# A four-layer network on one core: moving work about in the stretch ahead of a 512-step recurrence

## The reference, cut to what matters

```python
# layer 0: which 5120 entries of a batch's 512 x 512 are largest, as ones
adj = fside * cond[:, None, :] * softmax(x) * 512 ** -0.5; adj[diagonal] = -inf
x = x + ones_at(top_k(adj.reshape(4, -1), 5120))        # ties go to the lowest index
# layer 1: attention, 16 heads of 32
scale, shift = split(cond @ W_emb + b_emb)
xn = rms_norm(x, g_norm) * (1 + scale) + shift
q, k, v = heads(xn @ W_qkv); q, k = rms_norm(q, g_q), rms_norm(k, g_k)
o = softmax(q @ k.T * 32 ** -0.5) @ v
x = x + o + o @ W_out
# layer 2: a GRU over the 512 rows, first state cond
x = x + gru(cond, x, W_ih, W_hh, b_ih, b_hh)
# layer 3: linear sampling of x along the features at places given by cond
x = x + sample(x, cond)
```

## Time and profile before

| | |
|---|---|
| median of 3 timed runs | 2341.22 us (2340.92 to 2341.77) |
| profiled execution: its time, its span | 2339.34 us, 2337.6 us |
| TensorE busy | 93% of the span |
| VectorE, ScalarE, GpSimd busy | 67%, 54%, 22% |
| granted TensorE clock | 0.991 of full over the span |
| x of batch 0 in | 6.32 us |
| first ranking (L956) | 40.03 us |
| last bound of the search done | 136.90 us |
| first projection of batches 0 to 3 | 169.19, 318.59, 471.48, 625.85 us |
| first step of the recurrence | 808.98 us |

### The profile page before, as it was taken

The page is one execution under the profiler, slowest core; times in us unless marked ns, Lnnn a source line. Parts: engine busy times, 40 slices in busy tenths (PEclk is TensorE's granted clock), DMA queues, the critical chain, the costliest instruction groups (busy, mean ns, idle before and its releaser), DMA issues.

```text
span 2337.6 us, 132042 instructions
## 1 busy us (share of the span) xinstructions
PE 2184.3 (93%) x56213; PEld 1850.2 (79%) x56213; DVE 1562.3 (67%) x7116; ACT 1272.9 (54%) x5557; POOL 506.9 (22%) x2267
## 2 busy tenths in 40 slices
PE   3778999898988999999999999999999999999998
PEld 2664655545545699999999999999999999999886
DVE  7986866778668456666666666666666667666665
ACT  5754946747548454566544445445454555444443
POOL 2001121121120122233222222222222222222221
PEclk9999999999999999999999999999999999999999
DMA  5000000010010000000000000000000000000000
GB/s 200 3 2 0 1 1 1 1 55 1 1 54 1 19 5 5 5 5 5 5 5 5 9 9 5 9 9 5 9 5 10 10 5 9 10 5 14 9 5 21
DMA packets 8404, 31.58 MB, mean 14 GB/s; under 512 B 836, under 2 KB 904, under 8 KB 7560
## 3 DMA queue, kind: packets, MB, share of 16 engines
q1 hardware_dynamic: 7392, 23.07, 2.6%
q10 hardware_dynamic: 424, 0.07, 0.0%
HBM read 18.94 MB, written 4.19 MB: 10 GB/s over the span
## 4 chain that ended last, share of the span: by engine, by line
PE 79%; DVE 12%; ACT 5%; issue 3%; POOL 0%; DMA 0%; ACTq 0%; DVEq 0%; POOLq 0%
PE psum L1710 49%; PE psum L1644 8%; PE psum L1479 5%; PE psum L1555 4%; PE psum L1573 3%; PE psum L1539 3%; PE psum L1519 2%; PE psum L1671 2%; DVE region_cols L994 2%; DVE region_cols L978 2%; DVE top L1135 1%; PE psum L1498 1%; PE psum L1457 1%; ACT region_rows L666 1%; PE psum L1588 1%
## 5 line engine op out<-in xcount | busy, mean ns | idle before, releaser
L1710 PE MATMUL psum<-parts0A,region_w_hh 128*128 128x40 f16 x12288 | 428.6, 181 | 7.9 <-DVE parts0A L1351 6.2
L1710 PE MATMUL psum<-parts1A,region_w_hh 128*128 128x40 f16 x12288 | 428.0, 181 | 6.7 <-DVE parts1A L1351 6.5
L1710 PE MATMUL psum<-parts1B,region_w_hh 128*128 128x40 f16 x12288 | 427.2, 181 | 1.3 <-issue 0.3
L1710 PE MATMUL psum<-parts0B,region_w_hh 128*128 128x40 f16 x12288 | 426.7, 181 | 0.6
L1710 PEld LDWEIGHTS psum<-parts0A,region_w_hh 128*128 128x128 f16 x12288 | 378.2, 96 | 44.3 <-DVE parts0A L1351 11.2
L1710 PEld LDWEIGHTS psum<-parts1A,region_w_hh 128*128 128x128 f16 x12288 | 377.6, 96 | 42.6 <-DVE parts1A L1351 11.6
L808 ACT ACTIVATE mixA<-rzA 128x8 f32<-128x8 f32 x512 | 110.8, 216 | 534.8 <-DVE rzA L1306 534.7
L1710 PEld LDWEIGHTS psum<-parts1B,region_w_hh 128*128 128x128 f16 x12288 | 361.6, 96 | 5.0 <-DVE parts1B L1351 1.8
L1710 PEld LDWEIGHTS psum<-parts0B,region_w_hh 128*128 128x128 f16 x12288 | 361.7, 96 | 3.5 <-DVE parts0B L1351 1.2
L486 POOL TENSOR_SCALAR lineA<-lineA 128x8 f32<-128x8 f32 x512 | 122.2, 239 | 845.0 <-DVE lineA L1342 845.0
L1306 DVE TENSOR_REDUCE rzA<-psum 128x8 f32<-128x32 f32 x512 | 97.8, 191 | 249.4 <-PE psum L1710 248.0
(11 more groups left out here) (228 smaller groups left out, 3717.4 us busy)
## 6 DMA issues: line engine op xcount, KB each, us to landing
region_rows<-in_x_dram SPq DMA_DIRECT2D x4, 1024.0 KB, 12.7
out_dram<-region_w_b SPq DMA_DIRECT2D x16, 256.0 KB, 2.4
region_w_a<-in_L_cond_W_qkv_dram SPq DMA_DIRECT2D x1, 3072.0 KB, 23.3
region_w_hh<-in_L_cond_W_hh_dram SPq DMA_DIRECT2D x4, 768.0 KB, 6.5
region_w_a<-in_L_cond_W_ih_dram SPq DMA_DIRECT2D x1, 3072.0 KB, 10.1
region_cond<-in_cond_dram SPq DMA_DIRECT2D x2, 1024.0 KB, 7.1
region_cols<-in_L_cond_W_emb_dram SPq DMA_DIRECT2D x1, 2048.0 KB, 19.0
region_w_out<-in_L_cond_W_out_dram SPq DMA_DIRECT2D x1, 1024.0 KB, 21.6
```

The costliest lines, as they stand in the source:

```text
L1710: made = e.matmul(k.slots(bank)[:, :, ch, :, 0:2], k.w16[:, 2 * read + c, part, NC * "rzn".index(g) + 2 * half + ch], k.parts[now][read][: ...
```

## The change

Ten pieces, all ahead of the recurrence:

1. `pe_embed` makes the embedding as rows (4 x 1024) with 8 program products of 512 columns, ahead of the first count; ScalarE copies them (`act_embed`) behind batch 2's keys and ahead of batch 3's; the first sum of a count waits for these copies. After the search eight transposes bring them into the old columns.
2. On SP's queue the condition rows move behind x of batch 1.
3. `dve_prepare` is split: its first three operations come ahead of the ranking, the nine scale operations behind the last masks of the search. GpSimd's all-reduce moves behind all the diagonals of v.
4. The first mask compares v with the pivot itself, in place of `side` with zero, so that only the later count waits for Sign; its prefix sums come ahead of the quota, `dve_scales` between them; and VectorE does the four last adds in place of GpSimd.
5. One-column activations (`act_table`) bring table loads forward: Sqrt behind the signs, Exp in each attention ahead of the last two turned copies, Sigmoid ahead of the recurrence.
6. `pe_columns` runs in pairs of blocks: raw, raw, normalised, normalised.
7. The diagonals have a place for each batch, and those of batches 1 to 3 are made in unit 2 of the attention before.
8. In batch 0 the value products of tiles 2 and 3 move behind the other products, each ahead of a turn of halves, and VectorE copies both behind its last low halves.
9. In batches 1 to 3 the last output product is cut in two, with the first scores between the halves, and VectorE's last output add comes behind the first maximum.
10. Batch 2's prefix sums wait for batch 1's normalised transposes, whose diagonals lie in the same place.

```diff
 def sp_program(e, k):
     e.dma_start(k.x[:, 0], ...)
-    e.dma_start(k.cond_rows.rearrange("p b d -> p (b d)"), ...)
     for b in range(1, B):
+        if b == 2:
+            e.dma_start(k.cond_rows.rearrange("p b d -> p (b d)"), ...)
         e.dma_start(k.x[:, b], ...)
...
@@ act_program
         if b:
             act_keys(e, k, b - 1, NT)
+    act_embed(e, k)
     act_keys(e, k, B - 1, NT // 2)
     act_search(e, k)
...
+    act_table(e, k, B, ACT.Sqrt)
     e.wait_ge(s["gt_sign"], B)
     act_row_powers(e, k, 0)
...
+def act_table(e, k, i, function):
+    e.activation(k.warm[:, i:i + 1], k.ones[:, 0:1], function)
+
+def act_embed(e, k):
+    for half in range(2):
+        e.wait_ge(s["emb_products"], half + 1)
+        e.activation(k.emb_rows[:, half * D:(half + 1) * D], k.banks[4 + half][0:B, :], ACT.Copy).then_inc(s["emb_rows"], 1)
...
@@ dve_program
     dve_row_max(e, k, 0)
-    dve_prepare(e, k)
     dve_row_max(e, k, 1)
...
     dve_mask(e, k, 3)
+    dve_prepare_most(e, k)
     dve_search(e, k)          # now calls dve_prepare behind its last mask
...
-    dve_mask_equal(e, k, 0); dve_mask_prefix(e, k, 0); dve_mask_quota(e, k, 0); dve_mask_taken(e, k, 0)
-    dve_scales(e, k)
+    dve_first_mask(e, k)
...
+def dve_first_mask(e, k):
+    dve_mask_equal(e, k, 0)
+    for t in range(NT):
+        e.tensor_tensor_scan(k.prefix[:, t], k.eq[:, t], ...).then_inc(s["prefix"], 1)
+    dve_scales(e, k)
+    dve_mask_quota(e, k, 0)
+    for t in range(NT):
+        e.wait_ge(s["quota"], 8)
+        e.wait_ge(s["prefix"], t + 1)
+        e.scalar_tensor_tensor(k.eq[:, t], k.prefix[:, t], k.quota[:, 0, t:t + 1], k.eq[:, t], ALU.is_le, ALU.mult).then_inc(s["taken"], 1)
+        e.scalar_tensor_tensor(k.x[:, 0, t], k.side[0][:, t], 0.0, k.x[:, 0, t], ALU.is_gt, ALU.add).then_inc(s["prefix"], 1)
+        e.wait_ge(s["taken"], t + 1)
+        e.wait_ge(s["prefix"], NT + t + 1)
+        e.tensor_tensor(k.x[:, 0, t], k.x[:, 0, t], k.eq[:, t], ALU.add).then_inc(s["masked"], 1)
...
@@ dve_attention
     if b:
         dve_out_adds(e, k, b - 1, (2,))
+    dve_maxima(e, k, b, 0)
+    if b:
         dve_out_adds(e, k, b - 1, (3,))
-    for n in range(AHEAD):
-        dve_maxima(e, k, b, n)
+    dve_maxima(e, k, b, 1)
...
+        if n == 2 and b + 1 < B:
+            dve_diagonals(e, k, b + 1)
...
@@ pe_program
     e.transpose(k.bank(7, VEC_ROWS), ...).then_inc(s["vec"], 1)
+    pe_embed(e, k)
     pe_search(e, k)
-    pe_embed(e, k)
+    pe_embed_columns(e, k)
...
 def pe_embed(e, k):
+    for half in range(2):
+        for c in range(NC):
+            made = e.matmul(k.banks[4 + half][0:B, :], k.condT[:, :, c], k.w_emb[:, c, half * D:(half + 1) * D], ...)
+        made.then_inc(s["emb_products"], 1)
...
@@ pe_attention
-        pe_project(e, k, b, t, (1, 2))
+        pe_project(e, k, b, t, (1, 2) if values_in_turn(b, t) else (1,))
         pe_turn_stack(e, k, b, t - 1, 0)
     if b:
         pe_out_matmuls(e, k, b - 1, (0,))
+    else:
+        pe_project(e, k, b, NT - 2, (2,))
     pe_turn_stack(e, k, b, NT - 2, 1)
     if b:
         pe_out_matmuls(e, k, b - 1, (1, 2))
+    else:
+        pe_project(e, k, b, NT - 1, (2,))
     pe_turn_stack(e, k, b, NT - 1, 0)
     pe_turn_stack(e, k, b, NT - 1, 1)
     if b:
-        pe_out_matmuls(e, k, b - 1, (3,))
-    for n in range(AHEAD):
-        pe_scores(e, k, b, n)
+        pe_out_matmuls(e, k, b - 1, (3,), range(0, 2))
+    pe_scores(e, k, b, 0)
+    if b:
+        pe_out_matmuls(e, k, b - 1, (3,), range(2, NC))
+    pe_scores(e, k, b, 1)
```

More of the change, by code:

```diff
@@ L275, in layout @@
         self.xT = view("cols", 0, FP32, NC, B, S)
-        self.diagonal = view("work", 24, FP32, NT, P)
+        self.diagonal = [view(*place, FP32, NT, P) for place in (("work", 24), ("w_hh", 12), ("rows", 4), ("rows", 12))]
         self.qk = view("work", 0, FP32, NT, QK, DH)
@@ L695, in act_attention @@
     act_stack(e, k, b, NT - 1, 1)
+    act_table(e, k, b, ACT.Exp)
     act_turn_stack(e, k, b, NT - 1, 0)
@@ L773, in act_gru @@
     s = k.sem
+    act_table(e, k, B + 1, ACT.Sigmoid)
     e.wait_ge(s["hh_scale"], 8)
@@ L1054, in dve_row_scales, with dve_diagonals @@
     e.reciprocal(k.row_rms[:, b], k.row_rms[:, b]).then_inc(s["row_rms"], 1)
+def dve_diagonals(e, k, b):
+    s = k.sem
+    for t in range(NT):
+        e.tensor_scalar(k.diagonal[b][:, t], k.ident[:], k.row_rms[:, b, t:t + 1], None, ALU.mult).then_inc(s["diagonals"], 1)
 def dve_columns(e, k, b):
@@ L1063, in dve_columns @@
         e.wait_ge(s["gt_sign"], B)
-    for t in range(NT):
-        e.tensor_scalar(k.diagonal[:, t], k.ident[:], k.row_rms[:, b, t:t + 1], None, ALU.mult).then_inc(s["diagonals"], 1)
     if b == 0:
+        dve_diagonals(e, k, b)
         e.wait_ge(s["row_power"], NT)
@@ L1507, in pe_out_matmuls @@
     for m in ms:
-        if b < B - 1:
+        if cs[0]:
+            pass
+        elif b < B - 1:
             n = NT * (b + 1)
@@ L1517, in pe_out_matmuls @@
             e.wait_ge(s["exp"], 2 * len(UNITS) * B)
-        for c in range(NC):
+        for c in cs:
             made = e.matmul(k.bank(m, S), k.w_out[:, c, m * P:(m + 1) * P], k.oT[:, c], start=(c == 0), stop=(c == NC - 1))
-        made.then_inc(s["w_out"], 1)
+        if cs[-1] == NC - 1:
+            made.then_inc(s["w_out"], 1)
 def pe_scores(e, k, b, n):
```

104 lines of the change are left out of this document (69 added, 35 removed).

## The result

The changed kernel takes 2316.89 us (median of 4 runs, 2313.34 to 2317.88) against 2341.07 (2339.71 to 2341.77) beside it: 0.9895 of the time before, interval 0.9878 to 0.9912. Forecast were 2312 and 2305 to 2322. Its profiled execution took 2313.34 for a span of 2311.6, 26.0 less than that of before.

What follows compares the result with a forecast made beforehand. The recurrence's products at L1710 (49% of the chain) bound the kernel, so gains lie only ahead of it: -3.2 - 6.3 - 2.3 - 9.4 + 0.9 - 8.7 = -29.0 from 2341.2, giving 2312 us; own range 2307 to 2317, with rivals 2305 to 2322.

Steps and rivals of the forecast that it cites:

- Start: Up to the first ranking: earlier weights but early embedding products, batch 3's mask at 34.8 instead of 38.18; -3.2 us.
- Search to first projection: From the search's last bit to the first projection: mask, table load and columns earlier, -6.3 us, bounds -8 and -3.5.
- The mask's term: Between search and first projection: the first mask's last tile at 154.4 against 158.2, -3.7 us, bounds -4.5 to -2.4.
- the table load's: Between squares and root after the search: ScalarE's 1.28 us load, issued behind the signs, leaves the way; -1.3.
- the columns' -1.3: First transposes to first projection: raw and normalised groups without waits, one group partly slow, 6.3 us instead of 7.56.
- Batch 0: Batch 0's projections to scores: value products fill TensorE's waits, scores start at 228.5; -2.3 us, bounds -3.5 and -0.5.
- Changes of batch: Three changes, divide to projection: early diagonals let raw and normalised groups run without a gap; -9.4 us, bounds -11 and -5.5.
- The forecast's lower bound: Changes of batch: if only the wait for diagonals goes, some 1.8 us each, -5.5 for the three.
- Starts of scores: Three starts, last output product to weighted values: half product ahead and early Exp, -2.9 each, -8.7 us, bounds -11 and -5.9.
- +0.9 for the diagonals: Unit 2 of batches 0 to 2: VectorE's four small early-diagonal passes cost 0.9 us in all, bounds 0 and 2.6.
- The signs named in advance: Profile marks: first projection near 159.7, weighted values at 15 to 15.5; wrong if products exceed 12 us or recurrence grows over 2.
- rival 4: Recurrence: gain lost through shifted code and other alignments, break-even 57 ns a step over 512 steps, 2341 us; chance 0.01.

Runs made afterwards that it cites:

- keys_first: Changed kernel with batch 3's keys ahead of the embedding copies on ScalarE; ranking 2.83 us behind the embedding products, against 3.77.
- embed_late: Changed kernel with the row-form embedding products back behind the search; ranking at 34.66, first transposes 1.55 us later, recurrence starts at 782.82.
- filled: Changed kernel plus 12 unread TensorE products ahead of batch 0's columns; ratio to the kernel before 0.9891 (0.9875 to 0.9906).
- before_again: The kernel before, unedited, profiled a second time; recurrence starts at 809.76 and lasts 1534.54 us, against 808.98 and 1528.62.
- v_in_turn: Changed kernel with batch 0's value products and copies of tiles 2 and 3 back in turn; projection to scores 62.08 us, against 60.96.
- late_exp: Changed kernel without any early Exp table load; last output product to weighted values 16.76, 15.90, 16.13 us against 15.74, 15.74, 15.30.
- late_diag: Changed kernel with diagonals of batches 1 to 3 built at the change of batch again; first change 9.00 us, against 7.35.
- v_one_late: Changed kernel with only tile 3's value product late and no early Exp in batch 0; ratio to the kernel before 0.9898 (0.9882 to 0.9913).
- pool_adds: Changed kernel with the first mask's four last adds back on GpSimd; first transposes 0.97 us later, 18.92 behind the last bound.

## Why the prediction was right, point by point

**Start, -3.2 forecast, -2.7 measured** at the ranking. The products came at 23.7 and took 9.85 (forecast 24.0 and 9), the mask at 35.23 (34.8). The step held; keys_first shows what it overlooked: of two things that ScalarE had to do at 33.6, the copies went first, and the ranking waited 0.9 longer for it. The forecast didn't part the products' new place from their new form; embed_late shows that the place gains nothing in this order.

**Search to first projection, -6.3 forecast, -4.3 measured.** The mask's term was right (-3.7, measured -3.36), and so was the table load's (-1.3, measured -1.07, from the last add to the first normalised products). The mis-sized term is the columns' -1.3: "TensorE has been at work since 154.5, so that I cost one group of L1457 slow in part (1.5)". Its parts as listed (1.5, three at 0.9, two at 0.45, 0.9) come to 6.0, not 6.3, so that the list itself gives -1.6. Two groups were slow, 3.78 for the pair, and the stage took 7.70 against 7.56 before. filled gave back 2.1 of it. By the other profiles one pair sizes it badly: 8.26 in before_again, 6.16 to 7.71 in changed kernels without fillers. The rule cited in the prediction from the Trainium skill ("TensorE: Matmul & The Clock Gate", Part 1), that the throttled state is the default and activity releases it, agrees with filled, where TensorE was at work up to the columns, and with embed_late, where it had rested 8.6 us just ahead of them and the stage took 7.63.

**Batch 0, -2.3 forecast, -0.7 measured.** "Two value products (7.0 together) go into these gaps": they did, and the wait of 5.20 before 226.10 went down to 1.48. What the step left out is the gap that they left behind: 3.76 at 196.21, and after it 1.50 and 4.94 at the slower level, 1.7 more than 1.06 and 3.65. v_in_turn puts the worth of the piece at 1.1 to the scores, and at 0.4 to the first weighted values. late_exp puts the price of the early load at 0.2: as forecast, it brings nothing here.

**Changes of batch, -9.4 forecast, -9.6 measured** (-3.74, -2.09 and -3.73). late_diag divides it: 1.65 a change for the diagonals, and a rest of 2.1, 0.4 and 2.1. The 0.4 is the pairs of blocks: with a second raw group run inside it, the wait of 1.83 for the diagonals is 1.39 in late_diag. The first normalised products of the first change, in before and in late_diag:

```profile
310.94 1.47 PE L1457 MATMUL psum<-region_work,region_rows 128*128 128x128 f32 x8 [1.83 <-DVE region_work L1065]
```

```profile
300.79 2.05 PE L1543 MATMUL psum<-region_w_hh,region_rows 128*128 128x128 f32 x16 [1.39 <-DVE region_w_hh L1120]
```

The 1.65 more in the first and third change is TensorE's level in before, which fell there behind the wait, and not in the second (windows of before, columns as in the last section):

```profile
307.50:318.60 11.10, 8.41 (x61) 7.96 (x57) 5.18 (x12) 3.71 (x5) 0.00 (x0) 0.85 0.00 0
462.04:471.48 9.44, 6.75 (x60) 6.32 (x57) 5.18 (x12) 3.71 (x5) 0.00 (x0) 1.00 0.01 2
```

In late_diag all three run at full clock although the wait is there; why it fell in two of three places before isn't shown. The forecast's lower bound, 1.8 for the wait alone, was the right size for the diagonals.

**Starts of scores, -8.7 with +0.9 for the diagonals, measured -2.4, -2.2 and -3.6.** The sum is near, -8.2 for -7.8. In batch 1 the split is worth 1.6, Exp 1.0, and the diagonals cost 0.4. "exponential at +3.9 instead of +7.2" was +4.1, the second pair's at +6.5 was +6.8, and the weighted values came at +15.7, just outside the 15 to 15.5 that were named for them, and inside in batch 3. What didn't bear out is that an early load saves its 1.28: the second unit's maximum, 1.30 late, hides most of it in batch 2 and part of it elsewhere (late_exp). The load was 1.28 long in each of these kernels, with 0.02 or less between it and a function that was ready, ahead of it too where ScalarE had been at work (143.07 in after). So the 2.66 that the Trainium skill gives a switch ("ScalarE: Activation LUTs", What ACT_TABLE_LOAD costs) has no place here.

**What wasn't forecast:** batch 3's way from projection to scores, 74.69 before, was 71.58 in after and 71.57 in v_one_late, but 72.85 to 74.54 in the nine others with the same order there; 1.4 of the gain in after's profile is up to the last output product, differs between executions of one kernel, and is luck. So is part of the total: the named stretches gave 25.3 of their 29.0, these tiles 1.3 more, the recurrence took some back, and the median of 2316.89 lies 0.1 inside the forecast's own 2307 to 2317.

**The signs named in advance.** Products of 9.85, under 12; no table load between squares and root, nor ahead of the first exponential, nor in the recurrence after its start; no pause of TensorE over 1 us behind unit 2; the last add 3.4 earlier, not 3.7; first projection 162.36, not 159.7; recurrence 0.7 longer in the first pair. By the other profiles the limit of 2 us set for it was smaller than what the same kernel does from one execution to the next (1529.28, 1536.49; before, 1528.62, 1534.54), so one pair could not have told anything. The forecast of 0 for the recurrence was wrong all the same, by some 2 us or more: the medians and the usual step say so above. It is what rival 4 named, shifted code, in a small size; that the code's place is the cause isn't shown.

## What to carry to other kernels

Undo each piece alone and read the stretch it touches, not the time: pieces worth 1 to 4 us were clear in single profiles, while five timed executions showed nothing of 3 us. But keep the sum of the stretches beside the time: where the time gains less each time, the stretch that nobody touched has changed. A load or copy moved off the way is worth what the next wait behind it leaves, so follow the chain to the second and third unit before giving it its full length. And when work leaves an engine whose clock falls at rest, price what runs behind the gap at the slower level too.

## What the runs showed of the hardware that was not expected

- The record of the granted clock starts with its first change. In before it reads 1.00 from the start, also at 161.63, where eight normalised products took 2.08 instead of 1.06; in after the same counts stand under 0.54 and 0.50, once wide products at 23.7 have lifted it. Windows of before and of after (us, busy and count of PE, PEld, DVE, ACT, POOL, then PEclk, DMA share, GB/s):

```profile
60.00:158.00 98.00, 76.17 (x1769) 67.91 (x1769) 92.68 (x146) 69.03 (x315) 5.63 (x4) 1.00 0.01 3
```

```profile
60.00:158.00 98.00, 66.61 (x1668) 58.03 (x1669) 93.02 (x163) 69.89 (x309) 0.00 (x0) 0.50 0.01 3
```

  So a mean clock of 0.991 before and 0.969 after is no slower chip: embed_late, where nothing wide runs before 131.26, reads 0.990.
- The same 16 wide instructions took 8.31 to 9.93 in different executions and places: how soon the level rises behind like work isn't the same each time, and that alone moved the start and the columns by up to 1.5.
- VectorE's pass over 512 elements took more than twice as long beside GpSimd's add as alone (1.64 and 0.68). In pool_adds each of the three such passes ended 0.54 behind the add it had begun beside, as if held until its end, and an add begun during VectorE's pass before (0.74) took 0.4 longer: the two took turns.
